# A decoder layer on one core: the self-attention's matrix products reordered in phases of eight, with three score banks

## The chip, the cores and the metric

The kernel runs on one core of a Trainium2 chip. The time is device microseconds of one execution; the runs' median is compared. Before the change three runs gave 863.48, 863.65 and 865.51 us.

The engines of a core work through their own instruction streams and wait for each other by semaphores: PE (TensorE) multiplies matrices into PSUM, DVE (VectorE), ACT (ScalarE) and POOL (GpSimd) work elementwise, SP issues DMAs. PSUM has eight banks of 128 x 512 float32. POOL is given no PSUM operand in this kernel.

## The reference

A decoder layer over x (2 x 1024 x 256), 16 heads of 16:

```python
q, k, v = (x @ W.T for W in (Wq, Wk, Wv))                 # split over the heads
attn = softmax(q @ k.T / sqrt(16)) @ v                     # 1024 keys, no mask
x = layernorm(x + attn)
x = layernorm(x + cross_attention(x, ctx, mask))           # 77 keys
x = layernorm_affine(x + top2_experts(x))                  # 8 experts, 256 -> 512 -> 256
```

The change lies in the second line, and in the projections of q and k that run beside it.

## The kernel before, in words

**Units.** The self-attention is cut into 16 units: batch (2) x group of four heads (4) x half of the queries (2, 512 each). Each unit has 32 steps, one for each key tile of 128 (8) and head (4). A step is a score matmul (`scores`, L534, bfloat16 parts stacked to 98 rows), an exponential on ACT (`exps`, L1488) and a value product (`values`, L542, float32). Value products of four heads go to the four 32-column strips of the array and add up in bank 6; four heads of one key tile form a group. The values carry a column of ones, so the softmax's sum comes with them.

**Maxima.** The softmax needs each query's maximum first. For each unit PE computes 16 pairs of matmuls of 128 queries x 1024 keys (`max_pair`, L515) into `quad`, banks 0 to 3, two banks to a pair, and DVE reduces each pair (`reduce_max`, L952). After the 16th, DVE negates (`negate`), PE turns the result (`turn_negmax`, L528, into bank 7), DVE copies it (`keep_negrows`, L965), SP puts it into two rows of `qstack` (`load_negmax`), and the score matmul subtracts it. Pairs run ahead: during unit u, PE computes pairs 8 to 15 of unit u+1 and 0 to 7 of unit u+2.

**Results.** When a unit's value products are in bank 6, ACT copies it (`outT`, L1571), PE turns it (`turn_out`, L721, into bank 7) and DVE divides by the sums (`normalise`, L1214).

**Late projections.** q and k come from 16 projections ("jobs", `project`, L466) of which 8 run early and one in each of units 1 to 8, into bank 7. Each is split in three bfloat16 parts: ACT copies the high one (`high`), DVE makes the rest, the middle and the low one (`split_rest`, `split_mid`, `split_low`). SP stores the parts (`store_parts`) and loads them as stacks for two units at a time (`load_group`), after the odd unit's last value product.

**Order.** It is written out by hand in PE's `unit` (L724): eight times a group of four scores, four maximum matmuls (two pairs) and four value products of the group before. Scores alternate between banks 4 and 5; `probs` holds 8 tiles. The maximum matmuls alternate with the scores one by one.

After unit 15, whose stream already holds the first cross-attention work (`turn_x1`, `project_q2`, `scores2`), come cross-attention and the experts. Meanwhile POOL has split the experts' weights from the end of the last projection on.

Names in the profile: `bank` stands for banks 4 to 7 and `quad` for 0 to 3.

Of the kernel before, what the change touches and what calls it, by code (L numbers as in the profile page):

```python
# [13 lines left out]
P = 128  # L14
# [14 lines left out]
PR = 8  # L29
# [45 lines left out]
def build(nc, t):  # L75

    with ExitStack() as ctx:
# [154 lines left out]
        neg_loaded = sem("neg_loaded")  # L232
        scores_ready, probs_ready, probs_used = map(sem, ("scores_ready", "probs_ready", "probs_used"))
# [43 lines left out]
        START2 = (2, 3, 5)  # L277

# [11 lines left out]
        QK_BANK = [(4, 5, 0, 1)[n % 4] if n < EARLY_JOBS else 7 for n in range(QK_JOBS)]  # L290

        def job_of(u):
            n = EARLY_JOBS - 1 + u
            return n if EARLY_JOBS <= n < QK_JOBS else None

# [20 lines left out]
        def _(sp):  # L316
# [22 lines left out]
            def store_parts(n):  # L339
# [3 lines left out]
                for part in range(3):  # L343
                    if part == 0:
                        sp.wait_ge(hi_done, n + 1)
                    elif part == 1:
# [45 lines left out]
            def sp_unit(it, k, last):  # L392
# [64 lines left out]
        def _(pe):  # L457
            def project(n, c):
# [7 lines left out]
                mm = pe.matmul(bank[QK_BANK[n]], w_in[("wq", "wk")[w]][:, c, half * P:half * P + P], xT[:, c, g * 512:g * 512 + 512],  # L466
# [41 lines left out]
            def max_pair(u, k, p, halves=(0, 1)):  # L508

                slot, half, j, qt = unit_slot(k), k % 2, p // 4, p % 4  # L510
                if 0 in halves:
                    pe.wait_ge(max_taken, u * 16 + p + 1)
                q = qstack[slot][0:MAXROW, half, j, qt * P:qt * P + P]
                for e in halves:
                    mm = pe.matmul(bank[2 * (p % 2) + e], q, kstack[slot][0:MAXROW, j, e * 512:e * 512 + 512],  # L515
# [4 lines left out]
            def turn_negmax(u, k, first=False):  # L520
                if first:
                    pe.wait_ge(v_done, V_JOBS)
                else:
                    pe.wait_ge(o_normed, u)
                if u and job_of(u - 1) is not None:
                    pe.wait_ge(rest_done, job_of(u - 1) + 1)
                pe.wait_ge(neg_parts, u + 1)
                pe.transpose(bank[7].bitcast(BF16)[0:32, 0:P], negparts[:, k % 2, :], ident16[:, :]).then_inc(neg_turned, 1)  # L528

            def scores(u, k, i):  # L530

                slot, half, kt, j = unit_slot(k), k % 2, i // 4, i % 4
                pe.wait_ge(probs_ready, u * STEPS + i + 1)
                mm = pe.matmul(bank[4 + i % 2], kstack[slot][0:KROWS, j, kt * P:kt * P + P],  # L534
# [4 lines left out]
            def values(u, k, i):  # L539
                kt, j = i // 4, i % 4  # L540
                pe.wait_ge(probs_ready, u * STEPS + i + 3)
                pe.matmul(bank[6][32 * j:32 * j + VW, :], v_all[:, u // 2, kt, j, :], probs[:, i % PR, :],  # L542
                          start=(kt == 0), stop=(kt == KT - 1), skip_group_check=True).then_inc(probs_used, 1)
# [24 lines left out]
            turn_negmax(0, 0, first=True)  # L568
# [3 lines left out]
            for i in range(3):  # L572
# [17 lines left out]
            def project_q2(g, half):  # L590
                if half == 0:
                    pe.wait_ge(x1T_done, g * 2 + 2)
                for c in range(C2):
# [115 lines left out]
            pairs = [(1, p) for p in range(AHEAD, 16)] + [(2, p) for p in range(AHEAD - 1)]  # L709
            when = [pairs[2 * m:2 * m + 2] for m in range(KT)]  # L710
            pairs0 = [(1, p) for p in range(AHEAD0, 16)] + pairs[16 - AHEAD:]
            when0 = [pairs0[3 * m:3 * m + 3] for m in range(4)] + [pairs0[12 + 2 * m:14 + 2 * m] for m in range(4)]
            SPREAD = (1, 2, 1)
            TURN, TURN0 = 5, 6

            def turn_out(u):
                pe.wait_ge(o_copied, u + 2)
                pe.wait_ge(neg_rows, min(u + 2, UNITS))
                pe.wait_ge(o_normed, u + 1)
# [1171 lines left out]
```

## Time and profile before

| | |
|---|---|
| median of 3 runs | 863.65 us |
| span of the profiled execution, first to last instruction | 856.1 us |
| what lies around the span, median less span | 7.5 us |
| PE busy | 737.2 us (86%) |
| DVE busy | 638.0 us (75%) |
| ACT busy | 488.0 us (57%) |
| POOL busy | 305.1 us (36%) |

The execution that was profiled has no time of its own beside its span in the results; the median stands for it. Busy is the time in which an engine has an instruction in flight, so a share of 86% does not say that PE streams at its peak. A row of the timeline merges equal instructions that follow each other; its bracket gives the idle time before it and which engine's work ended that idle time. In a row with x2 the second starts inside the time given. PEclk is the granted TensorE clock as a share of 2.4 GHz.

### The profile page before, as it was taken

What the parts mean: (1) busy time and instruction counts of PE and PEld (TensorE: products, weight loads), DVE (VectorE), ACT (ScalarE), POOL (GpSimd) and SP (SyncE); (2) the same over time, 40 slices, a digit from 0 to 9 for tenths busy, and PEclk for the clock granted to TensorE, in tenths of its full rate; (3) what the DMA queues carried; (4) which work ended last, traced back from release to release, by engine and by line L of the source; (5) the groups of instructions that cost most, each with busy time, mean ns of one, the idle gap of its engine ahead of it and who ended that gap; (6) DMA issues with size and microseconds to landing.
All of it is one profiled execution on the core that took longest, in us unless ns stands there. A gap on an engine that the chain in (4) does not pass through costs nothing.

```text
span 856.1 us, 14502 instructions
## 1 busy us (share of the span) xinstructions
PE 737.2 (86%) x4572; PEld 355.0 (41%) x4572; DVE 638.0 (75%) x1087; ACT 488.0 (57%) x982; POOL 305.1 (36%) x249
## 2 busy tenths in 40 slices
PE   6789999999999999999988889899869898789800
PEld 3442222222222222222223356566657676567600
DVE  3488888888888888777884779897927656589765
ACT  2225677777777677776776553442335666457622
POOL 8000600000000398890002465555732474444311
PEclk9898999999999999999999999897979999899965
DMA  7746040030401699883000090000141332413121
GB/s 197 185 111 159 5 94 20 19 77 17 93 20 35 147 254 276 249 258 115 2 1 1 17 375 2 0 2 1 49 148 40 92 128 89 145 48 95 58 99 49
DMA packets 51170, 80.72 MB, mean 94 GB/s; under 512 B 16469, under 2 KB 35416, under 8 KB 49690
## 3 DMA queue, kind: packets, MB, share of 16 engines
q1 hardware_dynamic: 37065, 44.91, 19.2%
q0 software_dynamic: 9952, 31.29, 11.9%
q10 hardware_dynamic: 4080, 3.61, 1.8%
q8 instruction: 40, 0.66, 0.3%
q14 instruction: 33, 0.26, 0.1%
HBM read 48.21 MB, written 33.11 MB: 95 GB/s over the span
## 4 chain that ended last, share of the span: by engine, by line
PE 57%; DVE 20%; DMA 6%; issue 5%; ACT 4%; POOL 4%; SPq 2%; DVEq 1%; ACTq 0%; POOLq 0%
PE bank L542 12%; PE bank L534 12%; PE quad L515 11%; PE quad L861 5%; DVE rowmax L952 5%; PE bank L878 5%; DMA kstack<-k_parts 3%; PE quad L612 2%; PE bank L466 2%; DVE hl L1182 2%; ACT probs L1488 2%; POOL x_sorted L1778 2%; DVE sc L1055 1%; DVE max L1062 1%; DMA qstack<-q_parts 1%
## 5 line engine op out<-in xcount | busy, mean ns | idle before, releaser
L952 DVE TENSOR_REDUCE rowmax<-quad 128x1 f32<-128x1024 f32 x256 | 303.1, 1219 | 75.9 <-PE quad L515 75.4
L1488 ACT ACTIVATE probs<-bank 128x512 f32<-128x512 f32 x512 | 284.2, 595 | 115.1 <-PE bank L534 112.2
L534 PE MATMUL bank<-qstack,kstack 98*128 98x512 bf16 x512 | 194.1, 387 | 11.7 <-ACT probs L1488 10.0
L515 PE MATMUL quad<-kstack,qstack 96*128 96x512 bf16 x512 | 177.7, 387 | 15.5 <-DVE rowmax L952 6.7
L861 PE MATMUL quad<-xbT,w 128*128 128x128 bf16 x1104 | 119.6, 224 | 22.5 <-DVE hl L1182 16.1
L542 PE MATMUL bank<-probs,v_all 128*32 128x512 f32 x1024 | 139.0, 611 | 0.0
L534 PEld LDWEIGHTS bank<-qstack,kstack 98*128 98x128 bf16 x512 | 49.0, 97 | 191.7 <-ACT probs L1488 162.8
L861 PEld LDWEIGHTS quad<-xbT,w 128*128 x1104 | 91.3, 100 | 53.1 <-issue 38.3
L1612 ACT ACTIVATE hid<-quad,b 128x128 f32<-128x128 f32 x184 | 52.6, 370 | 59.6 <-PE quad L861 58.0
L515 PEld LDWEIGHTS quad<-kstack,qstack 96*128 96x128 bf16 x512 | 48.5, 99 | 77.0 <-DVE rowmax L952 39.3
L1832 POOL DMA_INDIRECT y_tokens<-ysb,dest x46 | 47.3, 1029 | 82.8 <-DVE ysb L1196 75.1
L1730 POOL DMA_DIRECT2D w1raw<-in_w x8 | 6.5, 806 | 188.6 <-PE bank L466 188.6
L878 PE MATMUL bank<-w,hh 128*128 x184 | 71.8, 392 | 1.5 <-DVE hl L1182 1.4
L1182 DVE TENSOR_TENSOR hl<-hid,hh 128x512 bf16<-128x512 f32 x46 | 42.9, 933 | 25.2 <-ACT hh L1618 25.2
L1766 POOL TENSOR_TENSOR lnv<-lnv,power 128x4 f32<-128x4 f32 (+1 forms) x14 | 19.1, 1367 | 110.2 <-DVE lnv L1007 110.2
L1786 POOL TENSOR_TENSOR sc<-sc,max 128x1232 f32<-128x1232 f32 x15 | 34.4, 2291 | 55.1 <-DVE max L1062 55.1
L878 PE MATMUL bank<-w,hl 128*128 x184 | 51.4, 279 | 0.0
L1509 ACT ACTIVATE pT<-bank 128x512 f32<-128x512 f32 (+1 forms) x48 | 23.6, 524 | 41.3 <-PE bank L630 41.1
L612 PE MATMUL quad<-kbd,q2T 128*128 128x308 f32 x128 | 43.5, 475 | 1.3 <-DVE sc L1055 1.3
L644 PE MATMUL bank<-pT,vbd 128*128 128x512 f32 (+3 forms) x100 | 37.6, 528 | 2.4 <-ACT pT L1509 2.4
L1055 DVE TENSOR_TENSOR sc<-quad,cap 128x1232 f32<-128x1232 f32 x16 | 22.8, 1428 | 22.4 <-PE quad L612 22.4
L1778 POOL DMA_INDIRECT x_sorted<-attn_all,rowof x32 | 32.8, 1025 | 12.1 <-issue 8.0
(181 smaller groups left out, 984.6 us busy)
## 6 DMA issues: line engine op xcount, KB each, us to landing
xb<-x_sorted SPq DMA_DIRECT2D x46, 129.0 KB, 2.3
x_sorted<-blank POOLq DMA_DIRECT2D x6, 774.0 KB, 9.1
w1raw<-in_w POOLq DMA_DIRECT2D x8, 512.0 KB, 6.0
w2raw<-in_w POOLq DMA_DIRECT2D x8, 512.0 KB, 6.4
w_split<-w1two POOLq DMA_DIRECT2D x8, 512.0 KB, 5.7
w_split<-w2two POOLq DMA_DIRECT2D x8, 512.0 KB, 4.4
w<-w_split SPq DMA_DIRECT2D x16, 256.0 KB, 5.0
w<-w_split SPq DMA_DIRECT2D x4, 1024.0 KB, 11.7
```

What stands on the lines that cost most here:

```text
L515: mm = pe.matmul(bank[2 * (p % 2) + e], q, kstack[slot][0:MAXROW, j, e * 512:e * 512 + 512], start=True, stop=True)
L534: mm = pe.matmul(bank[4 + i % 2], kstack[slot][0:KROWS, j, kt * P:kt * P + P], qstack[slot][0:KROWS, half, j, :], start=True, stop=True)
L542: pe.matmul(bank[6][32 * j:32 * j + VW, :], v_all[:, u // 2, kt, j, :], probs[:, i % PR, :], start=(kt == 0), stop=(kt == KT - 1), skip_gr ...
L612: mm = pe.matmul(bank[e][:, 0:4 * SC], q2T[:, half, i * P:i * P + P], kbd[:, g // 2, half, 4 * (e % 2):4 * (e % 2) + 4, :].rearrange("p h ...
L861: mm = pe.matmul(bank[m % 3][:, fc * P:(fc + 1) * P], w1[half][c][fc][:, bass.ds(at, P)], xbT[:, m % 3, 2 * part + c, :], start=(k == 0), ...
L878: mm = pe.matmul(bank[Y_BANK[m % 2]][:, 0:n], a[:, m % 2, fc, :], w2[fc][:, bass.ds(at * (2 * D // P), n)], start=(step == 0), stop=(fc == ...
L952: dve.tensor_reduce(rowmax[:, k % 2, p:p + 1], quad[:, 2 * (p % 2):2 * (p % 2) + 2, :].rearrange("p a n -> p (a n)"), AX_X, ALU.max).then_ ...
L1182: dve.tensor_tensor(hl[:, m % 2, :, :], hid[:, m % 2, :, :], hh[:, m % 2, :, :], ALU.subtract).then_inc(hl_done, 1)
L1488: act.activation(probs[:, i % PR, :], bank[4 + i % 2], ACT.Exp, scale=INV4).then_inc(probs_ready, 1)
L1612: act.activation(hid[:, m % 2, fc, :], bank[m % 3][:, fc * P:(fc + 1) * P], ACT.Relu, bias=b1[:, bass.ds(e, 1), fc]).then_inc(hid_done, 1)
L1778: pool.indirect_dma_start(xs[h], bass.IndirectOffsetOnAxis(ap=rowof[:, j, n:n + 1], axis=0), xsend[:, n, :], None).then_inc(scattered[h], 16)
L1832: pool.indirect_dma_start(ys[h], bass.IndirectOffsetOnAxis(ap=dest[:, m % XB:m % XB + 1], axis=0), ysb[:, m % YB, :], None, bounds_check=2 ...
```

## The change

- PE's unit is four phases in place of eight groups. A phase is eight times a score and one half of a maximum pair (in unit 0 at first a whole pair), then the value products of two key tiles, eight in one block. `probs` holds 12 tiles.
- Scores rotate over banks 4, 5 and 7, and three run ahead of the exponentials (LEADING).
- `turn_out` and `turn_negmax` now write to banks 2 and 0. So that they fit into the rotation of the pairs, pairs 2 to 9 use the other two banks than before, from unit 2 on: `turn_out` comes after pair 9, `turn_negmax` after pair 1, and pairs 10 and 2 wait for one reduction more.
- A late projection runs in one piece after score 14, in the score bank that is next in turn. ACT copies its bank twice, as the bfloat16 part and in float32 (`keep_job`), and POOL makes the rest, the middle and the low part, before its masks and before the experts' weights.
- A value product raises `probs_used` once for four.
- SP loads the next stacks after the odd unit's last score matmul instead of its last value product.
- The cross-attention work in unit 15 has new places in the order.

```diff
-PR = 8
+PR = 12
+PHASES, PER = 4, 8
+LEADING = 3
+JOB_AT = 14
...
+        SCORE_BANKS = (4, 5, 7)
+        NEG_BANK, OUT_BANK = 0, 2
...
+        def score_bank(u, i, job=False):
+            before_it = sum(job_of(v) is not None and (v, JOB_AT) < (u, i) for v in range(u + 1))
+            return SCORE_BANKS[(u * STEPS + i + before_it + job) % len(SCORE_BANKS)]
...
# SP, load_group of the next stacks
-                    sp.wait_ge(probs_used, u * STEPS + (STEPS + PR))
+                    sp.wait_ge(scores_ready, u * STEPS + STEPS)
...
# PE
             def max_pair(u, k, p, halves=(0, 1)):
+                shifted = u >= 2 and 2 <= p < 10
                 if 0 in halves:
-                    pe.wait_ge(max_taken, u * 16 + p + 1)
+                    if u >= 2 and p == 3:
+                        pe.wait_ge(neg_rows, u)
+                    elif u >= 2 and p == 11:
+                        pe.wait_ge(o_normed, u)
+                    else:
+                        pe.wait_ge(max_taken, u * 16 + p + 1 + (u >= 2 and p in (2, 10)))
...
+            def turn_negmax(u, k):
...
+                elif u < UNITS - 1:
+                    pe.wait_ge(max_taken, u * 16 + 19)
...
+            def turn_out(u):
+                pe.wait_ge(o_copied, u + 2)
+                if u < UNITS - 2:
+                    pe.wait_ge(max_taken, u * 16 + 43)
...
+            def scores(u, k, i):
+                behind = i - JOB_AT if job_of(u) is not None else 0
+                if behind == LEADING:
+                    pe.wait_ge(raw_done, job_of(u) - EARLY_JOBS + 1)
                 else:
+                    pe.wait_ge(probs_ready, u * STEPS + i + 1 + (0 < behind < LEADING))
...
+            def values(u, k, h):
+                if h == 0:
+                    pe.wait_ge(o_copied, u + 1)
+                pe.wait_ge(probs_ready, u * STEPS + PER * h + PER + LEADING)
+                for i in range(PER * h, PER * h + PER):
+                    kt, j = i // GH, i % GH
+                    mm = pe.matmul(bank[6][32 * j:32 * j + VW, :], v_all[:, u // 2, kt, j, :], probs[:, (u * STEPS + i) % PR, :],
+                                   start=(kt == 0), stop=(kt == KT - 1), skip_group_check=True)
+                    if j == GH - 1:
+                        mm.then_inc(probs_used, GH)
...
# PE, ahead(i)
                         scores(u, k, i)
+                        if i == JOB_AT and job_of(u) is not None:
+                            pe.wait_ge(probs_ready, u * STEPS + i + 2)
+                            for c in range(C2):
+                                project(job_of(u), c)
...
# PE, unit
+                    max_pair(u + a, k + a, p, (e,))
+                    if (a, p, e) == (1, 9, 1) and u:
+                        turn_out(u - 1)
+                    elif (a, p, e) == (2, 1, 1):
                         turn_negmax(u + 1, k + 1)
...
+                for h in range(PHASES):
+                    for s in range(PER):
+                        ahead(PER * h + LEADING + s)
+                        share = -(-len(halves) // (PER * (PHASES - h) - s))
+                        for a, p, e in halves[:share]:
+                            pair(a, p, e)
+                        halves = halves[share:]
...
+                    values(u, k, h)
...
# ACT, after exponential 14 of a unit with a job
+            def keep_job(u):
+                act.activation(parts[:, n % RING, 0, :], bank[job_bank(u)], ACT.Copy).then_inc(hi_done, 1)
...
+                act.activation(rest[:, n % 2, :], bank[job_bank(u)], ACT.Copy).then_inc(raw_done, 1)
...
# POOL
+            for n in range(EARLY_JOBS, QK_JOBS):
+                m, raw, three = n - EARLY_JOBS + 1, rest[:, n % 2, :], parts[:, n % RING, :, :]
+                pool.wait_ge(raw_done, m)
+                pool.tensor_tensor(raw, raw, three[:, 0, :], ALU.subtract).then_inc(late_rest, 1)
+                pool.wait_ge(late_rest, m)
+                pool.tensor_copy(three[:, 1, :], raw).then_inc(late_mid, 1)
+                pool.wait_ge(late_mid, m)
+                pool.tensor_tensor(three[:, 2, :], raw, three[:, 1, :], ALU.subtract).then_inc(late_low, 1)
```

## Rows read from the trace of the kernel before

**Rows 1.** The page: chain that ended last, shares of the span by engine

```profile
PE 57%; DVE 20%; DMA 6%; issue 5%; ACT 4%; POOL 4%; SPq 2%; DVEq 1%; ACTq 0%; POOLq 0%
```

**Rows 2.** Busy time by window: us, busy (instructions), PEclk, DMA share, GB/s

```profile
61.58:92.81 31.23, 29.40 (x140) 7.82 (x141) 24.48 (x24) 19.42 (x35) 5.58 (x3) 0.89 0.50 113
92.81:275.68 182.87, 179.51 (x960) 53.34 (x959) 150.56 (x169) 132.13 (x239) 8.35 (x5) 1.00 0.19 42
275.68:303.68 28.00, 25.73 (x138) 7.60 (x137) 23.64 (x24) 18.88 (x34) 11.19 (x10) 1.00 0.64 153
303.68:453.11 149.43, 141.78 (x785) 39.75 (x784) 118.77 (x146) 109.25 (x199) 75.23 (x64) 1.00 0.55 160
404.31:428.70 24.39, 23.91 (x134) 6.79 (x133) 19.91 (x21) 18.17 (x33) 0.00 (x0) 1.00 0.01 1
453.11:487.68 34.57, 30.20 (x138) 11.05 (x136) 18.62 (x27) 21.75 (x37) 12.06 (x8) 0.95 0.00 1
```

**Rows 3.** Timeline, unit 13: start, us, engine line op; x2 merges two

```profile
423.21 0.39 PE L534 MATMUL bank<-qstack,kstack 98*128 98x512 bf16 x1
...
423.64 2.17 ACT L1488 ACTIVATE probs<-bank 128x512 f32<-128x512 f32 x4 [0.71 <-PE bank L534]
...
423.88 0.59 PE L515 MATMUL quad<-kstack,qstack 96*128 96x512 bf16 x2
...
424.30 2.36 DVE L952 TENSOR_REDUCE rowmax<-quad 128x1 f32<-128x1024 f32 x2 [0.53 <-PE quad L515]
...
424.78 0.39 PE L534 MATMUL bank<-qstack,kstack 98*128 98x512 bf16 x1
...
425.10 1.06 PE L542 MATMUL bank<-probs,v_all 128*32 128x512 f32 x8
...
426.10 0.39 PE L534 MATMUL bank<-qstack,kstack 98*128 98x512 bf16 x1
```

**Rows 4.** Timeline, unit 0

```profile
77.50 0.60 PE L515 MATMUL quad<-kstack,qstack 96*128 96x512 bf16 x2
...
78.14 3.49 DVE L952 TENSOR_REDUCE rowmax<-quad 128x1 f32<-128x1024 f32 x3 [0.41 <-PE quad L515]
...
79.42 0.60 PE L515 MATMUL quad<-kstack,qstack 96*128 96x512 bf16 x2 [0.45 <-DVE rowmax L952]
```

**Rows 5.** Timeline, ends of units 13 and 15

```profile
427.50 1.07 PE L542 MATMUL bank<-probs,v_all 128*32 128x512 f32 x8
...
428.70 0.60 ACT L1571 ACTIVATE outT<-bank 128x512 f32<-128x512 f32 x1 [0.51 <-PE bank L542]
...
486.60 0.14 PEld L542 LDWEIGHTS bank<-probs,v_all 128*32 128x32 f32 x2 [0.61 <-ACT probs L1488]
...
487.68 0.60 ACT L1571 ACTIVATE outT<-bank 128x512 f32<-128x512 f32 x1 [1.14 <-PE bank L542]
```

**Rows 6.** Chain of waits, unit 1: start us, us, what

```profile
95.42 0.44 PE bank L721 x4
...
99.51 0.42 DVE attn_all L1222
...
101.95 0.86 PE bank L466 x2
```

**Rows 7.** POOL's early split, by line (ns: min/median/max); DVE's cast, timeline of unit 8

```profile
L1692 POOL TENSOR_TENSOR parts<-rest,parts x4: 1148/1156/1158, 14.1 to 18.7; 128x512 bf16<-128x512 f32 x4
...
295.61 2.30 DVE L926 CAST parts<-rest 128x512 bf16<-128x512 f32 x1
```

**Rows 8.** Waits of PE (310 to 480); chain, units 9 to 10; POOL's timeline

```profile
PE quad L515 <- DMA kstack<-k_parts: 2.5, 2, 1.4
...
328.94 0.60 SPq L362
...
331.73 11.20 DMA kstack<-k_parts
...
450.60 1.68 POOL L1766 TENSOR_TENSOR lnv<-lnv,power 128x8 f32<-128x8 f32 x1 [62.99 <-DVE lnv L1007]
```

More of the change, by code:

```diff
@@ L567, in _ @@
             max_pair(1, 1, 0)
-            turn_negmax(0, 0, first=True)
+            turn_negmax(0, 0)
             for p in range(1, AHEAD0):
@@ L571, in _ @@
             pe.wait_ge(neg_loaded, 32)
-            for i in range(3):
+            for i in range(LEADING):
                 scores(0, 0, i)
@@ L706, in rank @@
                 mm.then_inc(ranks_ready, 1)
[L709 to L719, printed above, removed]
-                for qt in range(4):
-                    tr = pe.transpose(bank[7][:, qt * P:qt * P + P], outT[:, qt * P:qt * P + P], ident[:, :])
-                tr.then_inc(o_turned, 1)
+            pairs = [(1, p) for p in range(AHEAD, 16)] + [(2, p) for p in range(AHEAD)]
+            pairs0 = [(1, p) for p in range(AHEAD0, 16)] + [(2, p) for p in range(AHEAD)]
             def unit(it, k, last):
@@ new lines, in pair @@
+                    if (a, p, e) == (1, 9, 1) and u:
+                        turn_out(u - 1)
+                    elif (a, p, e) == (2, 1, 1):
+                        turn_negmax(u + 1, k + 1)
+                halves = [(a, p, e) for a, p in (pairs if u else pairs0) for e in range(2)]
+                for h in range(PHASES):
[5 more added lines that the diff above has]
+                        halves = halves[share:]
+                        if last and s == 3:
+                            if k == 2 and h == 2:
+                                turn_negmax(u + 1, k + 1)
+                            elif k == 3 and h == 0:
+                                turn_out(u - 1)
+                                turn_x1(0)
+                            elif k == 3 and h == 1:
+                                for half in range(2):
+                                    scores2(0, half)
@@ L777, in unit @@
                             pe.wait_ge(mask_step, MASK_STEPS)
-                        elif m in START2:
+                        elif h < 3:
                             for half in range(2):
-                                scores2(START2.index(m), half)
-                heads(KT - 1)
-                if not (last and k + 2 > 3):
-                    max_pair(u + 2, k + 2, AHEAD - 1)
-                ahead(STEPS + 2)
+                                scores2(h, half)
+                    values(u, k, h)
             for it in range(3):
@@ L951, in reduce_max @@
                 dve.wait_ge(max_ready, u * 16 + p + 1)
-                dve.tensor_reduce(rowmax[:, k % 2, p:p + 1], quad[:, 2 * (p % 2):2 * (p % 2) + 2, :].rearrange("p a n -> p (a n)"),
+                at = 2 * ((p + (u >= 2 and 2 <= p < 10)) % 2)
+                dve.tensor_reduce(rowmax[:, k % 2, p:p + 1], quad[:, at:at + 2, :].rearrange("p a n -> p (a n)"),
                                   AX_X, ALU.max).then_inc(max_taken, 1)
```

115 lines of the change are left out of this document (46 added, 69 removed).

## The prediction

> **What bounds the kernel now.** I read the page's chain that ended last first: TensorE (PE) holds 57% of it, VectorE (DVE) 20% [rows 1]. Then the stretches [rows 2]. Self-attention runs as 16 units from 61.6 to 487.7 us. A unit without a late projection takes 24.39 us (unit 13, 404.31 to 428.70), one with it 26.12 (units 1 to 7, 182.87 us for seven), and PE is busy in all but half a microsecond of each; DVE has 19.9 and 21.5 us of work in them, ScalarE (ACT) under 19. So the matmul stream seems the bound. The timeline says what the stream is made of and how close DVE is behind it. In a regular group of four score matmuls (S), four maximum matmuls (M, two make a pair) and four value products (V) [rows 3], S and M lie 0.22 us apart, V starts 0.32 after its S, and the next S is 1.00 after V starts. A V group thus costs 1.10, and the whole group 4 x 0.22 + 4 x 0.22 + 1.10 = 2.86; measured 2.89 (423.21 to 426.10). DVE takes up a pair 0.42 after the pair's second M starts (its second M at 423.88, the reduction at 424.30); two reductions take 2.36, that is 1.13 from start to start and 1.22 for the last. DVE rests for 0.53 per group. ACT starts an exponential 0.43 after its S and does four in 2.17: 0.525 apart, 0.60 long.
>
> The four quad banks hold two pairs, so the third of a burst waits until the first is reduced. Unit 0 has three pairs to a group and shows it [rows 4]: pair A is issued at 77.50 and 77.72, its reduction starts at 78.14 and ends at 79.36; pair C could go at 78.81 and goes at 79.42, 0.06 after that end. I use this spacing below.
>
> **Eight value products together.** Two groups of four now stand back to back. The last value product of the attention, alone because its exponential came late, ran from 486.60, and ACT could read its bank at 487.68 [rows 5]; after a full group of four that is 1.20 (427.50 to 428.70). So the four heads stream side by side, in about 0.86 us, 0.04 apart. The second four use the same columns of the array and must stream after the first: 0.10 entry + 0.14 stagger + 2 x 0.86 = 1.96, against 2.20 for two groups. Bounds: 1.82 (no stagger) and 2.20 (nothing saved). I take 1.96, since the stagger is in the row. TensorEngine Tiling in the Trainium skill (Key Properties) says that changing the tiling mode drains the engine. The trace agrees with its 0.32 in place of 0.22; that rule is on the change's side, though the lone transpose of the maxima, which used to lie against a V group, now pays two switches. TensorE: Matmul & The Clock Gate in the Trainium skill (The cost: per-tile semaphore tail) prices each increment at 26.3 ns; six fewer per block would give an estimate of 1.80 for it and a total near 871.
>
> **One phase of eight.** A phase is now S M eight times, then the block. Count from its first S; Sn is the phase's nth S, Mna and Mnb the two matmuls of pair n (0 to 3). M0b is at 0.66, so reduction R0 starts at 1.08, ends at 2.30; R1 starts at 2.21, ends at 3.43. M2a could go at 1.98 but needs R0: 2.35. Then S 2.57, M2b 2.79, S 3.01; M3a needs R1: 3.48. S 3.70, M3b 3.92, block 4.14, next phase 6.10. Without the wait it would be 3.52 + 1.96 = 5.48. R2 and R3 end at 4.56 and 5.69 and DVE then idles until 7.18, as no new pair can appear during the block. The cycle M0b - R0 - R1 - M3 - block - M0b is closed: 0.42 + 1.13 + 1.22 + 0.05 + 0.66 + 1.96 + 0.66 = 6.10. Two old groups take 5.78. This is my central claim: the longer block starves DVE and then the burst of four pairs outruns two buffers. Three score banks keep ACT clear: exponentials run from 0.42 every 0.525, and the eighth S needs the end of the fifth's, 3.12, before 3.70.
>
> **The transposes.** turn_out now sits between pair 1 and pair 2 in bank 2 and waits for R0: 2.35. It lasts 0.44, by the chain of waits [rows 6]: S 2.79. Pair 2 must now wait for R1, 3.48 (banks 0 and 1): S 3.70, M2b 3.92, S 4.14, M3a 4.36 (normalise follows R1 and ends with a product of 0.42 [rows 6], at about 4.15), S 4.58, M3b 4.80, block 5.02, end 6.98. turn_negmax has the same place in the third phase; its few tenths lie within the wait for R1, and keep_negrows (0.2) before M3a too: again 6.98. A unit is 6.98 + 6.10 + 6.98 + 6.10 = 26.16, against 24.39.
>
> **Late projections (units 1 to 8).** They now stand whole behind S14, the fourth S of the second phase, for 1.72 us (two times 0.86 [rows 6]). They need exponential 12 of the unit: start 1.61. M1b moves to 3.33, S to 3.55. ACT makes two copies where it made one, at 3.53 and 4.06 to 4.66, so the S behind them in that bank waits to 4.72; pair 3 waits for R1 (3.75 to 4.97, so 5.02), its neighbour S for ACT's exponential 15, 5.245. Block 5.69, end 7.65: 1.55 over a plain phase. Unit: 27.71, against 26.12. DVE loses its three splits, but it idles here anyway, so that is worth nothing, except in unit 8: there a cast took 2.30 us while GpSimd (POOL) ran, and the unit took 28.00, 1.88 more than its seven forerunners [rows 2, 7]. SBUF — State Buffer in the Trainium skill (Who interferes with whom) says a cast of DVE can be blocked by GpSimd and tensor_reduce on trn2 never is; the trace agrees (units 9 to 13 keep their length although POOL works through most of them). POOL's own splits: two subtractions of 1.15 [rows 7] and a cast no longer than that, under 3.5 us per unit, after which SP stores; the next reader is the stack load a unit later. POOL gets to its masks only after unit 8, and so to the experts' weights later, by the length of the masks and the shift of unit 8, together less than a unit and a half; it idles 62.99 us before its next work at 450.60 [rows 8], which covers that. Uncovered, the excess over 63 us would delay the cross-attention; I see none.
>
> **Stack loads.** SP now issues them once the unit's last S is issued, about 4.3 us before the unit's end, instead of after its last value products. The PE waits for kstack, 2.5 us in all in units 10 and 12 [rows 8], go: 14.0 us of issue and transfer (328.94 to 342.93) now lie under 4.3 + 6.98 + 6.10 = 17.4 us. On its queue the load is moved past nothing; the row of maxima follows it half a unit later. This gain is already in my 26.16.
>
> **Unit 0** has 42 halves. First phase: eight pairs at DVE's 1.13, first reduction about 64.2 (the granted clock of the unit was 0.89 on average, it began at the lower level, so issue is slow at first, but DVE sets the pace), pair 7's M at 71.2, end 73.7. Second, five pairs: 7.1, then 6.98 and 6.10: 93.9 against 92.7. +1.2. **Unit 14** lacks pairs in its second half, where ACT's 8 x 0.525 and the block set the length: 6.98 + 6.10 + 5.5 + 5.4 = 24.0. **Unit 15** has no M and holds the first cross-attention work. Laid out the same way, with ACT's exponentials, the two copies of x1T and of q2T and the last block of 1.96 behind the last exponential, it comes to 34.9 against 34.57 [rows 2].
>
> **Sum.** Units 1 to 7: 7 x 1.59 = 11.1. Unit 8: -0.3. Units 9 to 14: 5 x 26.16 + 24.0 = 154.8 against 149.43 [rows 2], +5.4. Units 0 and 15: +1.2 + 0.3. Total +17.7: the profiled span goes from 856.1 to 873.8. The median of the runs is 863.65; the 7.5 us around the span I leave alone. Forecast 881.4. A block of 1.82 takes 0.14 from some 62 phases, 8.7: 872.7. One of 2.20 adds 14.9: 896.3.
>
> **Rivals.** (1) Faster: PE's stream is the bound, as its busy time says. Place: pairs 2 and 3 of each phase; it decides if their waits are absent, so that phases average under 6.1 us (24.4 / 4). A unit is then 64 x 0.22 + 4 x 1.96 + 0.44 + 0.3 = 22.7, or 24.4 with a projection: 7 x 1.7 + 3.6 + 149.43 - 5 x 22.7 - 24.0 = 27.4 less, 836. For it: DVE has only 20 us of work in a 24 us unit. Against: unit 0's wait [rows 4] is this very pattern. (2) No change: waits half as long as laid out, paid for by the stack loads (2.5) and unit 8 (1.9): about 864. (3) The blocks save nothing, since the second four heads drain before loading: 896 or more; for it speaks only that no row shows eight together. (4) PE's clock, 1.00 in units 1 to 14 [rows 2], falls to 1.2 GHz in places because PE waits more (0.62 us in a plain phase). The 0.95 of unit 15 is such a dip; there PE was busy for 30.2 of 34.6 us, a share that the new units come near to. A unit wholly at 1.2 GHz would double its 22.7 us of issue, so one to two such units in all give 900 to 920.
>
> **Chances.** Forecast 0.75, (1) 0.10, (2) 0.04, (3) 0.08, (4) 0.03. About 0.3% is what a measurement can tell from no change. Faster 0.10, same 0.04, slower 0.86. Range 866 to 898: both bounds of the block, and some room below for terms laid out by hand; case 1 is left out.
>
> **What would show it.** In a plain phase M of pair 2 idles some 0.4 us and of pair 3 some 0.2 before a release by DVE's reduction, phases last 6.1 and 7.0, units 26.2 and 27.7; DVE idles about 1.5 us at each block; the kstack waits and the long cast are gone; a block starts the next S 1.86 after its own start. Wrong: units under 24.4, ACT named as releaser of most S, or blocks far from 1.86.

## The result, and the profile after

The changed kernel takes 888.0 us (median of 4 runs, 884.08 to 890.32), beside 863.57 for the kernel before (4 runs, 859.94 to 865.51). The ratio is 1.0289, 95% interval 1.0257 to 1.0321: slower by 24.4 us, where the forecast was 881.4, slower by 17.7. The profiled execution took 886.86 us, its span is 885.0.

First the page of the changed kernel: busy times, the chain that ended last, and three groups (busy us, mean ns of one | idle before, releaser).

```profile
PE 736.3 (83%) x4572; PEld 367.6 (42%) x4572; DVE 626.0 (71%) x1063; ACT 476.3 (54%) x990; POOL 330.4 (37%) x273
...
PE 51%; DVE 26%; issue 6%; DMA 5%; ACT 5%; POOL 3%; SPq 1%; DVEq 1%; ACTq 0%; another core or an unknown queue 0%; POOLq 0%
...
L976 DVE TENSOR_REDUCE rowmax<-quad 128x1 f32<-128x1024 f32 x256 | 299.6, 1218 | 109.6 <-PE quad L536 109.1
...
L536 PE MATMUL quad<-kstack,qstack 96*128 96x512 bf16 x512 | 194.5, 390 | 26.0 <-DVE rowmax L976 17.5
...
L580 PE MATMUL bank<-probs,v_all 128*32 128x512 f32 x1024 | 126.1, 611 | 2.2 <-ACT probs L1505 2.2
```

In the chain DVE goes from 20 to 26% and PE from 57 to 51% [rows 1]. On the page of the kernel before, the reductions idled 75.9 us and the maximum matmuls 15.5 us; now it is 109.6 and 26.0, and each names the other as releaser. Two engines that wait for each other by turns are a closed cycle, and neither one's busy share (83% and 71%) shows it. PE's busy time is what it was, 736 for 737.

The stretches, in the columns of [rows 2]: units 1 to 7, unit 9, units 10 to 14, unit 13, unit 15, and 3.2 us within unit 9.

```profile
94.27:288.63 194.36, 179.25 (x960) 59.10 (x959) 141.10 (x147) 128.18 (x245) 20.50 (x21) 1.00 0.19 42
...
316.40:346.15 29.75, 25.44 (x134) 7.81 (x133) 21.49 (x21) 17.33 (x33) 24.91 (x22) 0.94 0.78 209
346.15:474.93 128.78, 116.37 (x650) 36.65 (x649) 97.44 (x123) 86.67 (x165) 62.53 (x52) 1.00 0.54 155
425.25:451.42 26.17, 23.79 (x134) 7.61 (x133) 19.71 (x21) 17.44 (x33) 0.00 (x0) 1.00 0.01 1
474.93:509.96 35.03, 28.78 (x137) 11.32 (x135) 20.71 (x29) 19.80 (x36) 13.82 (x9) 0.95 0.00 1
342.30:345.50 3.20, 3.20 (x18) 0.60 (x16) 1.80 (x2) 0.80 (x2) 2.33 (x3) 0.50 1.07 269
```

Unit 13 takes 26.17 us (24.39 before), with DVE's work 0.2 us less and PE idle for 2.4 us instead of 0.5 [rows 2].

A plain phase, the answer to [rows 3], unit 13 of the changed kernel:

```profile
432.09 0.39 PE L568 MATMUL bank<-qstack,kstack 98*128 98x512 bf16 x1
...
433.18 4.62 DVE L976 TENSOR_REDUCE rowmax<-quad 128x1 f32<-128x1024 f32 x4 [1.35 <-PE quad L536]
...
433.85 0.38 PE L568 MATMUL bank<-qstack,kstack 98*128 98x512 bf16 x1
...
434.46 0.39 PE L536 MATMUL quad<-kstack,qstack 96*128 96x512 bf16 x1 [0.23 <-DVE rowmax L976]
...
435.12 0.38 PE L568 MATMUL bank<-qstack,kstack 98*128 98x512 bf16 x1
...
435.59 0.39 PE L536 MATMUL quad<-kstack,qstack 96*128 96x512 bf16 x1
...
436.34 1.92 PE L580 MATMUL bank<-probs,v_all 128*32 128x512 f32 x16
...
438.20 0.39 PE L568 MATMUL bank<-qstack,kstack 98*128 98x512 bf16 x1
```

Read the starts rather than the brackets. Without a wait a matmul follows its neighbour by 0.22. The first half of pair 2 follows by 0.61 (433.85 to 434.46), that of pair 3 by 0.47 (435.12 to 435.59): 0.64 us of waiting per phase, of which the bracket shows 0.23, since a matmul counts as busy for 0.38 and so hides what follows it. The block starts the next score 1.86 after its own start. The phase lasts 6.11 and DVE rests 1.35 ahead of it.

This is where the 22.3 us went by which the attention (to the last copy out of bank 6) is longer in these two traces (it ends at 487.68 and at 509.96):

| | before | after | more | forecast |
|---|---|---|---|---|
| unit 0, end | 92.81 | 94.27 | 1.5 | 1.2 |
| units 1 to 7 | 182.87 | 194.36 | 11.5 | 11.1 |
| unit 8 | 28.00 | 27.77 | -0.2 | -0.3 |
| units 9 to 14 | 149.43 | 158.53 | 9.1 | 5.4 |
| unit 15 | 34.57 | 35.03 | 0.5 | 0.3 |

Behind the attention the two kernels have the same code, which took 368.4 us before and 375.0 after. I don't put that down to the change: in the 14 traces of this study it took 368.1 to 378.6 us, and the kernels that ran together on a chip lie together (368.1 to 371.6 the first four, 377.1 to 378.6 the next four, 373.2 to 376.2 the next three), whatever was done to the attention. For single stages I therefore compare units, for totals the ratio of runs side by side.

### The profile page after: what moved, and what is told of

It reads as the page before. It is cut to its first block, busy times and chain, and to the rows that moved or that the text cites. A ratio compares the mean times of both kernels' runs of the same rounds, so it can differ in the third digit from the quotient of the medians.

```text
span 885.0 us, 14500 instructions
## 1 busy us (share of the span) xinstructions
PE 736.3 (83%) x4572; PEld 367.6 (42%) x4572; DVE 626.0 (71%) x1063; ACT 476.3 (54%) x990; POOL 330.4 (37%) x273
## 4 chain that ended last, share of the span: by engine, by line
PE 51%; DVE 26%; issue 6%; DMA 5%; ACT 5%; POOL 3%; SPq 1%; DVEq 1%; ACTq 0%; another core or an unknown queue 0%; POOLq 0%
DVE rowmax L976 14%; PE bank L580 13%; PE quad L536 9%; PE bank L568 8%; PE quad L884 5%; PE bank L901 4%; PE quad L654 2%; PE bank L481 2%; DVE hl L1206 2%; PE bank L686 2%; DMA qstack<-negrows 2%; POOL x_sorted L1817 2%; DMA qstack<-q_parts 1%; DVE sc L1079 1%; ACT probs L1505 1%
## 5 line engine op out<-in xcount | busy, mean ns | idle before, releaser
L976 DVE TENSOR_REDUCE rowmax<-quad 128x1 f32<-128x1024 f32 x256 | 299.6, 1218 | 109.6 <-PE quad L536 109.1
L1505 ACT ACTIVATE probs<-bank 128x512 f32<-128x512 f32 x512 | 270.2, 604 | 125.3 <-PE bank L568 123.7
L536 PE MATMUL quad<-kstack,qstack 96*128 96x512 bf16 x512 | 194.5, 390 | 26.0 <-DVE rowmax L976 17.5
L580 PE MATMUL bank<-probs,v_all 128*32 128x512 f32 x1024 | 126.1, 611 | 2.2 <-ACT probs L1505 2.2
L1739 POOL TENSOR_TENSOR rest<-rest,parts 128x512 f32<-128x512 f32 x8 | 9.3, 1157 | 255.9 <-ACT rest L1517 255.9
L580 PEld LDWEIGHTS bank<-probs,v_all 128*32 128x32 f32 x1024 | 27.1, 110 | 69.2 <-issue 48.2
L1817 POOL DMA_INDIRECT x_sorted<-attn_all,rowof x32 | 32.8, 1024 | 17.3 <-issue 5.5
```

What stands on the lines that cost most here:

```text
L536: mm = pe.matmul(bank[2 * ((p + shifted) % 2) + e], q, kstack[slot][0:MAXROW, j, e * 512:e * 512 + 512], start=True, stop=True)
L580: mm = pe.matmul(bank[6][32 * j:32 * j + VW, :], v_all[:, u // 2, kt, j, :], probs[:, (u * STEPS + i) % PR, :], start=(kt == 0), stop=(kt ...
L976: dve.tensor_reduce(rowmax[:, k % 2, p:p + 1], quad[:, at:at + 2, :].rearrange("p a n -> p (a n)"), AX_X, ALU.max).then_inc(max_taken, 1)
L1505: act.activation(probs[:, n % PR, :], bank[score_bank(u, i)], ACT.Exp, scale=INV4).then_inc(probs_ready, 1)
L1817: pool.indirect_dma_start(xs[h], bass.IndirectOffsetOnAxis(ap=rowof[:, j, n:n + 1], axis=0), xsend[:, n, :], None).then_inc(scattered[h], 16)
```

## The experiments

Two numbers carry most verdicts: the length of a plain unit (copy of bank 6 to copy of bank 6; of units 9 to 13 the shortest, so the one that nothing disturbed) and of a unit with a projection. Before they are 24.4 and 26.12, after 26.17 and 27.77. Undisturbed units repeat to a few hundredths of a microsecond within a trace and from one to the next, while totals vary by 0.5%.

### Is it the length of the block?

```diff
-PHASES, PER = 4, 8
+PHASES, PER = 8, 4
```

Everything else of the change stays: three banks, transposes in the rotation, splits on POOL, early load. (Unit 15's work is put at the same step numbers.)

> The changed kernel with blocks of four value products again (eight phases of four slots); three score banks, transposes in the rotation of the maximum, GpSimd's splits and the early stack loads stay. Theory T (the block of eight starves VectorE, and four pairs in a row then outrun the two pairs of quad banks): a plain stretch of eight slots falls from 6.11 to 2 x 2.86 = 5.72 us; turn_out and turn_negmax still wait about 0.6 for a reduction, so a unit is 6.75 + 5.72 + 6.5 + 5.72 = 24.7 without a projection and some 26.6 with one, instead of 26.17 and 27.77. Total near 866. Rival A (the transposes and their extra waits in the rotation are the loss, the block is innocent): units stay above 25.7, total above 880. Rival B (what is left is the late projection in one piece): only units 9 to 14 get near the old 24.4, units 1 to 8 stay near 27.7.

Measured: 858.38 us beside 858.84, ratio 1.0009 (0.9984 to 1.0034). Plain unit 24.47 (unit 13; units 9 to 12 took 24.70 to 25.36), projection unit 26.31. The theory had 24.7 and 26.6. The same groups of its page:

```profile
L977 DVE TENSOR_REDUCE rowmax<-quad 128x1 f32<-128x1024 f32 x256 | 302.0, 1220 | 89.5 <-PE quad L536 88.6
...
L536 PE MATMUL quad<-kstack,qstack 96*128 96x512 bf16 x512 | 192.6, 386 | 10.6 <-DMA qstack<-q_parts 7.1
...
L580 PE MATMUL bank<-probs,v_all 128*32 128x512 f32 x1024 | 137.5, 608 | 1.4 <-ACT probs L1506 1.4
```

The value products are busy for 11.4 us more (137.5 for 126.1), and yet the attention ends at 486.37, 23.6 us sooner: on the page no wait for reductions leads for the maximum matmuls any more (10.6 us of idle time, most of it for a transfer, for 26.0), and DVE idles 20 us less before its reductions (89.5 for 109.6). The block's length is the cause of the loss. One unit was odd: unit 8 took 32.25 us.

```profile
290.28 4.40 POOL L1748 TENSOR_SCALAR cap<-cap 128x1232 f32<-128x1232 int32 x1
290.42 4.30 DVE L984 TENSOR_SCALAR negparts<-rowmax 128x16 bf16<-128x16 f32 x1
...
296.12 0.29 PE L548 MATMUL quad<-ident,negparts 128*32 128x128 bf16 x1 [4.41 <-DVE rowmax L977]
```

A negation of 16 columns, 0.17 us by itself, stood for 4.30 beside a mask operation of POOL's, and PE idled 4.41 before `turn_negmax`, with the granted clock at 0.50 for the next 4 us. The bracket names the reduction, which had to wait for the negation; what held the negation is POOL's row. The experiments on POOL below follow this up.

### Is it DVE, or PE's stream?

```diff
# changed kernel; the same in the kernel before
-quad[:, at:at + 2, :].rearrange("p a n -> p (a n)")
+quad[:, at, :]
```

Each reduction reads 512 of the 1024 keys, so the maxima are of half the keys.

> The changed kernel with reductions over the first 512 of each pair's 1024 keys only (the second maximum matmul runs, its half is not read; a softmax may be shifted by any number). A reduction should take about 0.65 us in place of 1.22. Theory T: the waits of pair 2 and pair 3 go, a plain phase is 16 x 0.22 + 0.09 + 1.86 = 5.47 plus 0.1 that ScalarE takes = 5.57; with the transposes 6.2 and 5.9; unit 23.2, with a projection 24.8; unit 0 gains some 4; total 840 to 848. Rival (TensorE's own stream or its drains are the loss, VectorE is only a symptom): phases stay near 6.1, total above 875.

> The kernel before with the same half reduction. Theory T: TensorE's stream bounds it, VectorE is close behind only in unit 0 (0.6 per group) and around normalise (0.37): a unit goes from 24.4 to 24.0, unit 0 loses 4 to 5, total 851 to 857. So e2 must be FASTER than e3 by some 10 us: blocks of eight are worth their 0.25 us per phase once VectorE is out of the way. Rival (the block of eight gains nothing in itself): e2 and e3 equal, or e2 slower.

Measured: after 841.24 us, ratio 0.9814 (0.9777 to 0.9852); before 850.78, ratio 0.9900 (0.9859 to 0.9942). Plain units 23.28 and 24.08, projection units 25.44 and 25.72. With a reduction of 0.69 us the changed kernel waits no more for DVE in plain phases, and it wins by 0.80 a unit. So blocks of eight do save PE what they should, and the loss is DVE's. The totals say it less cleanly than the units: of the 8.5 us by which the attention ends sooner in the changed kernel (468.84 for 477.33), 5.3 are that units 9 to 12 of the kernel before were disturbed in its trace (unit 10 took 27.82) and those of the changed kernel hardly. Only the projection unit was off, 25.44 for 24.8 expected: 2.16 over the plain one, where the four matmuls take 1.72 of the stream. Two scores behind ACT's copies come 0.28 late together; what makes the rest stays open.

### What is the third score bank worth?

```diff
-LEADING = 3
+LEADING = 2
-        SCORE_BANKS = (4, 5, 7)
+        SCORE_BANKS = (4, 5)
```

> The changed kernel with two score banks (4 and 5), two scores ahead; blocks of eight and all else stay. Theory T: ScalarE's exponentials then hold each score back to 0.525 us, but VectorE's wait is the longer one: scores S0 to S7 of a phase at 0, 0.44, 1.08, 1.60, 2.13, 2.65, 3.18, 3.73, pair 3 at 3.51 as before, block at 4.2 instead of 4.14. A plain phase goes from 6.11 to about 6.15, total 886 to 892: the third bank buys almost nothing here. Rival (the third bank matters, without it the new order would lose more): each phase 0.3 or more longer, total over 905.

Measured: 904.84 us, ratio 1.0568 (1.0526 to 1.0611), a miss in the total. Beside a kernel before of 863.65 that ratio is 912.7, where 886 to 892 was expected and the rival had over 905. The waits of PE in this kernel from 94 to 500 us (in total, times, longest), which takes in the first 10 us of unit 15, then those of the changed kernel from 94 us to the end of unit 14:

```profile
PE quad L536 <- DVE rowmax L976: 13.0, 27, 0.6
PE bank L568 <- ACT probs L1505: 7.1, 22, 1.1
PE bank L568 <- ACT rest L1517: 4.2, 8, 0.5
```

```profile
PE quad L536 <- DVE rowmax L976: 14.7, 46, 0.6
PE quad L557 <- DVE rowmax L976: 7.5, 14, 0.5
PE quad L548 <- DVE rowmax L976: 6.4, 13, 1.1
PE bank L568 <- ACT probs L1505: 0.7, 3, 0.3
```

To the end of unit 14 alone the second row is 4.9 us in 19 waits. The plain phase is the same (6.12 us, for 6.11), as expected: DVE sets it. But the phase with `turn_out` grows to 7.38 and that with `turn_negmax` to 7.18 (both 6.98), units with a projection to 29.4, and unit 15, where ACT paces, to 41.2 (35.0). The attention ends at 531.55, 21.6 us later: so much is the third bank worth. The rival was right on the total, and wrong on the plain phases. I had priced the bank only where it does nothing.

### Can the starved start of a phase be filled?

```diff
-share = -(-len(halves) // (PER * (PHASES - h) - s))
+share = (2, 0, 2, 0, 2, 0, 0, 2)[s] if u else -(-len(halves) // (PER * (PHASES - h) - s))
```

The two halves of a pair follow each other, so a pair is ready 0.2 us after its first half.

> The changed kernel; from unit 1 on, the two matmuls of a maximum pair stand side by side in the phase of eight: S0 MM S1 S2 MM S3 S4 MM S5 S6 S7 MM, then the block of eight. Nothing is added or removed. Theory T (closed cycle: pair 0's second matmul, two reductions, pair 3, block): the second matmul of pair 0 moves from 0.66 to 0.44, so R0 runs 0.86 to 2.08, R1 1.99 to 3.21, pair 3 at 3.40, block at 3.94: a plain phase is 5.80 instead of 6.11, one with a transpose 6.75 instead of 6.98, a unit 25.1 instead of 26.17, one with a projection 26.7 instead of 27.77. In all some 15 us under the changed kernel: 1.011 to 1.016 of the kernel before. Rival (the loss is drains, or queueing in TensorE, whatever the order of the maximum's matmuls): units stay at 26.2, ratio 1.026 or more.

Measured: 883.58 us, ratio 1.0228 (1.0191 to 1.0265): the total misses the 1.011 to 1.016 that was worked out, and by itself its interval doesn't exclude the rival's 1.026. The units do exclude it. The plain phase is 5.81 (5.80 worked out), one with `turn_negmax` 6.75 (6.75), one with `turn_out` 6.87, and the plain unit 25.23, 0.1 over what was worked out. The attention ends at 501.65, 8.3 us sooner instead of some 15. The projection unit, 27.41, missed its 26.7: as in the half reduction, ACT's second copy holds a score (2.5 us in eight units, by the waits). Units 9 to 11 were disturbed (25.81 to 26.79), and unit 15 took 36.74. The plain phases confirm the cycle: shorten one of its links, from phase start to the first full pair, and each phase shrinks.

### Two repairs of the kernel before

```diff
# SP, before the next stacks: both kernels of this pair
-sp.wait_ge(probs_used, u * STEPS + (STEPS + PR))
+sp.wait_ge(scores_ready, u * STEPS + STEPS)
# POOL, before the weights: the second alone
-pool.wait_ge(qk_ready, QK_JOBS)
+pool.wait_ge(parts_done, QK_JOBS - 4)
```

> The kernel before with one part of the change: SP loads the next stacks after the odd unit's last score matmul instead of its last value product. Theory: PE's two waits for kstack at the middle of units 10 and 12 (2.5 us in the trace) go, nothing else moves: units 10 and 12 from 25.7 and 25.9 to 24.4, total 2 to 3 us less, ratio about 0.997. Rival: the loads then lie beside the experts' weights and delay the rows of maxima; no change.

> e6, and GpSimd starts on the experts' weights only when VectorE has made the last part of the last projection, some 10 us later. Theory: the cast of 2.30 us in unit 8 goes back to 0.42, unit 8 from 28.0 to 26.1; together with the early load 4 to 5 us less than before, ratio 0.994 to 0.996. Rival: GpSimd's later start pushes the weights' traffic onto something else, or another short VectorE cast is caught: the gain of e6 alone or less.

Measured: 865.19 us, ratio 1.0004 (0.9986 to 1.0022), and 862.76, ratio 0.9992 (0.9968 to 1.0015). In the traces both mechanisms work. The early load takes units 10 and 12 from 25.66 and 25.90 to 25.15 and 24.40 (24.4 was expected of both, and unit 11 gives 0.4 back). The later start of POOL takes unit 8 from 28.00 to 26.12. The attention ends 5.5 us sooner with both (482.22), 3.4 of it in units 8 to 14 and 1.2 in unit 15, where the granted clock was 1.00 instead of 0.95. Unit 9 is longer, 25.85 for 24.66. The totals can't be told from no change, and the 0.994 to 0.996 expected of both repairs lies just outside the interval: what 3 us in seven units do to the total these runs can't show, since the interval of twelve runs spans 4.

### Keeping POOL away from the negation

In the kernel with blocks of four, POOL's masks are first moved ahead of its late splits.

> e1 (the changed kernel with blocks of four) with GpSimd's masks ahead of its late splits, as in the kernel before, instead of behind them. In e1, unit 8 took 32.25 us: VectorE's negate of 128 x 16 took 4.30 beside GpSimd's first mask operation (4.40), and TensorE waited 4.41. Theory: this is a block between the two engines and goes with the order: unit 8 at 26.3, total 5 to 6 us under e1, so 0.992 to 0.995 of the kernel before, faster than both kernels. Rival: the wait has another cause (stores of the parts, the row's DMA) and unit 8 stays over 30.

Measured: 864.02 us, ratio 0.9981 (0.9961 to 1.0002). Unit 8 falls from 32.25 to 26.53, as expected (26.3). The total does not: 0.992 to 0.995 was expected, and the interval holds no change. Now unit 10 takes 27.73:

```profile
339.77 2.14 POOL L1785 TENSOR_TENSOR w2two<-w2raw,w2two 128x1024 bf16<-128x1024 f32 x1
339.95 1.99 DVE L986 SCALAR_TENSOR_TENSOR negparts<-rowmax,negparts 128x16 bf16<-128x16 f32 x1
...
343.13 0.23 PE L548 MATMUL quad<-ident,negparts 128*32 128x128 bf16 x1 [2.09 <-DVE rowmax L977]
```

The other half of the negation meets a weight split. So next the weight splits are spaced by the arrival of the maxima's rows:

```diff
                 for k in range(2):
+                    pool.wait_ge(neg_loaded, 32 * (10 + (2 * e + k) // 3))
+                    if k == 0:
+                        fill_sorted(e // FILLS, e % FILLS)
                     split_weights(e, k)
```

It is put into three kernels: blocks of four, the changed kernel itself (with the masks first), and the kernel before (with both repairs).

> The changed kernel with blocks of four and GpSimd's masks first, and GpSimd lets three weight splits (and the fill of the sorted rows) follow each time the maxima's rows have landed, from unit 9's on, in place of all in a row. Theory: what is left in units 10 to 12 over 24.47 us comes from DVE's negation standing behind a GpSimd split (1.99 us measured) and from the fills beside the rows' transfer. Then units 9 to 13 take 24.5 each, the last copy out of bank 6 ends at 479 us (483.4 without the spacing, 487.7 in the kernel before), ratio to the kernel before 0.988 to 0.994. Rival: the excess is the stacks' late arrival, which GpSimd doesn't touch: unit 10 stays at 27 us, attention ends at 482 to 484, ratio 0.996 to 1.000.

> The changed kernel (blocks of eight) with GpSimd's masks first and its weight splits spaced in the same way. Theory: unit 9's 29.75 us in the changed kernel is 26.2 of the plain unit and 3.6 of collisions with GpSimd (negation 1.95, the rows' transfer 6.90 in place of 1.7, the clock's dip behind it). It falls to 26.2, unit 10 to 26.2, the attention ends at 505 to 506.5 (509.96), the ratio to the kernel before is 1.020 to 1.026 (1.0289). Rival: it belongs to the change of kind of unit (the last projection's stacks): unit 9 stays above 28.

> The kernel before with the early load and the wait on the copies (as in the run with both), and GpSimd's weight splits spaced in the same way. Theory: unit 9 falls from 25.85 to 24.4, the attention ends at 480.8 (482.2 without the spacing, 487.7 in the kernel before), ratio to the kernel before 0.991 to 0.996. Rival: the spacing pushes GpSimd's work against the norm in unit 15: that unit grows from 33.35 and the ratio is 1.00.

Measured, all three beside 865.58 us: blocks of four 859.61, ratio 0.9932 (0.9909 to 0.9956); the changed kernel 883.98, ratio 1.0216 (1.0181 to 1.0250); the kernel before 861.67, ratio 0.9959 (0.9939 to 0.9979). All three ratios are in what the theory expected. The stages bear it out for the changed kernel only.

In the changed kernel units 9 to 13 are all 26.17 or 26.18 now: the collisions are gone (the negation takes 0.17 to 0.28 there), and the interval holds the ratio of the forecast (881.4 / 863.65 = 1.0206). Its attention ends at 507.16, a little past what I expected, because unit 15 took 36.6. There eight matmuls of the cross-attention took 3.51 us, where they had taken 2.24, with the granted clock at 0.81 from 494 to 501 on average; that is 1.3 of the 1.6 us by which the unit is longer than in the changed kernel (the first row is of this kernel's timeline, the second of the changed kernel's):

```profile
494.07 3.51 PE L654 MATMUL quad<-kbd,q2T 128*128 128x308 f32 x8
```

```profile
498.27 2.24 PE L654 MATMUL quad<-kbd,q2T 128*128 128x308 f32 x8
```

In the other two kernels unit 9 came right (24.60 and 24.41) and unit 10 did not (27.41 and 25.79), so their attention ended at 484.34 and 483.93, where 479 and 480.8 were expected, and no sooner than without the spacing (483.43 and 482.22). In blocks of four the unit and the end of the attention are about what the rival had named (27, and 482 to 484), though not for its reason, the stacks, while the ratio is the theory's. What made these two ratios better than those without the spacing (0.9981 and 0.9992) the traces of the attention don't show, and it can't be credited to the spacing. In blocks of four the weights' fetch was late, and the third split of its portion met the negation:

```profile
339.54 1.04 POOL L1783 CAST w2two<-w2raw 128x1024 bf16<-128x1024 f32 x1 [3.49 <-DMA w2raw<-in_w]
340.66 2.12 POOL L1785 TENSOR_TENSOR w2two<-w2raw,w2two 128x1024 bf16<-128x1024 f32 x1
...
341.16 1.66 DVE L984 TENSOR_SCALAR negparts<-rowmax 128x16 bf16<-128x16 f32 x1
```

One more kernel put only two splits into the first portion.

```diff
-pool.wait_ge(neg_loaded, 32 * (10 + (2 * e + k) // 3))
+pool.wait_ge(neg_loaded, 32 * (10 + (2 * e + k + 1) // 3))
```

> As the run with blocks of four and spaced splits, but only two splits stand in the first portion, so that the fetch of the weights, which came 4 us late in unit 10 beside the last stacks, no longer pushes the third split of a portion onto the negation (1.66 us in place of 0.17, PE idle 1.76 before the turn, and the granted clock at 0.79 behind it). Theory: unit 10 falls from 27.4 to 24.5 to 25.0, the attention ends at 481 to 482 (484.3), ratio to the kernel before 0.988 to 0.993. Rival: unit 10's excess is the stacks' transfer at a DMA share of 1.0: it stays above 26.5, ratio 0.993 to 0.996.

Measured: 855.17 us beside 858.52, ratio 0.9963 (0.9941 to 0.9984). The attention ends at 481.88, as expected; the total misses its 0.988 to 0.993, unit 10 is 25.70 for 24.5 to 25.0, and unit 12 is 25.96, where the negation took 1.83. In unit 10 the fetch was late again, by 5.08 us, and another split met the negation:

```profile
338.56 1.04 POOL L1783 CAST w1two<-w1raw 128x1024 bf16<-128x1024 f32 x1 [5.08 <-DMA w1raw<-in_w]
339.68 2.12 POOL L1785 TENSOR_TENSOR w1two<-w1raw,w1two 128x1024 bf16<-128x1024 f32 x1
340.25 1.58 DVE L984 TENSOR_SCALAR negparts<-rowmax 128x16 bf16<-128x16 f32 x1
```

A spacing by starts doesn't hold where a transfer decides when the split begins. A wait after each fetch, put between the negation's two ends, would; it wasn't tried. The two kernels of blocks of four with spaced splits are faster than the kernel before, by their intervals 0.2 to 0.9%, and so faster than the changed one; which of the two is better stays open.

## Why the prediction was right, and where its sizes were off

**The block, 1.96 with its entry.** Right: 0.31 from the matmul before (436.03 is the last maximum matmul's start in the phase shown, the block's is 436.34), less the usual 0.22, plus 1.86 to the next score: 1.95. The rival that the blocks save nothing is out. The estimate of 1.80 by the Trainium skill's increments (TensorE: Matmul & The Clock Gate, The cost: per-tile semaphore tail) is not borne out: six increments fewer left the block where the heads' stagger alone puts it.

**Pairs outrun DVE.** Right: the second pair of a phase to wait stood at 3.50 from the first score (3.48 forecast), the first at 2.37 (2.35), the phase is 6.11 (6.10), and DVE rests at each block. Halving the reduction removes the loss, blocks of four remove it, and closing the pairs shortens it by what the cycle says. That PE's stream is the bound (the fastest rival, 836) is excluded: its own condition, pairs 2 and 3 without waits, was nearly met only where half the keys were reduced (a plain phase of 5.45), at 841. The no-change rival needed waits half as long as laid out, and they are as long as laid out.

**The transposes.** Right. The third phase of unit 13, to its next score 6.98 later, rows of the changed kernel:

```profile
440.56 0.23 PE L548 MATMUL quad<-ident,negparts 128*32 128x128 bf16 x1 [0.44 <-DVE rowmax L976]
...
441.69 0.39 PE L536 MATMUL quad<-kstack,qstack 96*128 96x512 bf16 x1 [0.58 <-DVE rowmax L976]
...
445.18 0.39 PE L568 MATMUL bank<-qstack,kstack 98*128 98x512 bf16 x1
```

**Late projections.** Right to 0.06 per unit (27.77 for 27.71). The projection started 1.57 after its phase's first score (1.61), the phase took 7.70 (7.65). POOL's splits are hidden as forecast, 3.07 us, 216.93 to 220.00, though the negation at 219.50 took 0.53 beside them; PE did not wait for it.

```profile
213.75 1.98 PE L481 MATMUL bank<-xT,wqkv 128*128 128x512 f32 x4
...
215.77 0.60 ACT L1512 ACTIVATE parts<-bank 128x512 bf16<-128x512 f32 x1 [1.09 <-PE bank L481]
...
216.26 0.59 ACT L1517 ACTIVATE rest<-bank 128x512 f32<-128x512 f32 x1
...
216.93 1.16 POOL L1739 TENSOR_TENSOR rest<-rest,parts 128x512 f32<-128x512 f32 x1 [24.69 <-ACT rest L1517]
...
218.84 1.16 POOL L1743 TENSOR_TENSOR parts<-rest,parts 128x512 bf16<-128x512 f32 x1
```

**Units 9 to 14: the term that was too small,** +9.1 for +5.4. The working had 5 x 26.16 + 24.0. Three units gave 26.17 and unit 14 gave 23.51, but unit 9 took 29.75 and unit 10 26.75. I had looked for POOL's effect on DVE in one large cast, and concluded from a constant length of units 9 to 13 that POOL's weights hurt nothing. That reading was wrong: before, they took 24.66, 25.66, 24.41, 25.90 and 24.39. The stacks' waits are in units 10 and 12, but in unit 9 the negation took 0.95. The small negation was exposed to POOL all along, and the sum put this at nothing. In unit 9 of the changed kernel:

```profile
328.77 2.12 POOL L1783 TENSOR_TENSOR w2two<-w2raw,w2two 128x1024 bf16<-128x1024 f32 x1
328.98 1.95 DVE L983 TENSOR_SCALAR negparts<-rowmax 128x16 bf16<-128x16 f32 x1
...
332.32 0.23 PE L548 MATMUL quad<-ident,negparts 128*32 128x128 bf16 x1 [1.05 <-DVE rowmax L976]
...
341.10 0.39 PE L568 MATMUL bank<-qstack,kstack 98*128 98x512 bf16 x1 [1.40 <-DMA qstack<-negrows]
```

The row of maxima then took its transfer 6.90 us, by the chain of waits:

```profile
328.98 1.96 DVE negparts L983
...
334.16 6.90 DMA qstack<-negrows
...
342.72 3.35 PE bank L580 x16
```

It shares the DMA engines with the weights' traffic and the fill of the sorted rows, issued at 332.63, and PE waited 1.40 for it. Then the granted clock stood at 0.50, the lower level, for the 3.20 us shown with the stretches, and a block took 3.35 in place of 1.86. Negation, transfer and clock together are the 3.6 us over 26.16; the spaced kernel, in which all three are absent, gives 26.17. That POOL's work is their source is shown by it. By the unit's phases they divide so: the third, with the late negation, took 7.59 for 6.98, and the fourth, with the wait for the row and the slow block, 9.06 for 6.11. Which part of POOL's work slowed the transfer, and whether the clock would have fallen without the wait, stays open. The fourth rival, that the clock falls in places, thus happened here, but for 1.5 us, and once more in unit 15, where it had priced 20 or more.

**Unit 0, 15 and 8, the stack loads.** 1.5 for 1.2 (the working took unit 0's end before as 92.7, the trace has 92.81), 0.5 for 0.3, -0.2 for -0.3; the kstack waits are gone from PE's list. In unit 15 the agreement is luck. The working had a last block of 1.96 behind the last exponential, and in the changed kernel it took 3.45:

```profile
506.44 3.45 PE L580 MATMUL bank<-probs,v_all 128*32 128x512 f32 x16 [2.19 <-ACT probs L1505]
```

So the rest of the unit was 1.4 us shorter than laid out. The 34.57 before held a fall of the clock too (0.95 on average): in four other traces with the old order the clock was 1.00 and the unit took 33.35. Against these the changed kernel loses 1.7 us in unit 15, not 0.5.

**Beside the attention.** Of the 24.4 us between the medians 22.3 are the attention's, if the two traces stand for the medians. The rest is within what the same code varies by. My reading of the 7.5 us as what "lies around the span" was wrong: it is 1.9 in the changed kernel's profiled execution (886.86 less 885.0). The 7.5 must have been mostly the difference between a quick profiled execution and the median. It did no harm, because only differences were added to it.

## What to carry to other kernels

Before you lengthen an uninterrupted block on one engine, draw the cycle through its partner. Here four pairs followed a block and two pairs of banks stood between PE and DVE, so the time in which no new work for DVE appeared was paid in each phase, whatever the busy shares said. The same longer blocks with which the kernel lost 2.9% (2.2% with POOL kept away) were worth 0.8 us a unit once the partner was fast enough. And look for tiny instructions on the critical path of an engine that another one can block: give them a time when the other is quiet, or they can cost as much as its longest operation.

## What the runs showed of the hardware

- A DVE operation of 128 x 16 elements, float32 to bfloat16, took 4.30 us beside one POOL operation of 4.40 (blocks of four), and 1.95 and 1.99 beside splits of 2.12 and 2.14, as a TENSOR_SCALAR and as a SCALAR_TENSOR_TENSOR. Alone it takes 0.17. Two reductions beside the same POOL work took 2.36, as always (unit 9 of the changed kernel, 334.32). SBUF — State Buffer in the Trainium skill (Who interferes with whom) names kinds of operations that can block each other, says that the later one is held for the whole of the other's instruction, and excepts tensor_reduce on trn2; these rows agree. What I hadn't expected is how much this costs for one of 16 columns on the critical path.
- Two rows of maxima took 6.90 us to land in a stretch with a DMA share of 0.97 (unit 9 of the changed kernel, 334.16 to 341.05), and 1.7 in the median.
- The granted clock falls for a few microseconds, and not always at the same place in otherwise equal units: unit 15's eight matmuls took 2.24 and 3.51 in two kernels with the same instructions there. PE had idled shortly before each of these falls (1.21 before these eight, 1.40 in unit 9 of the changed kernel, 4.41 in unit 8 with blocks of four), but the same 1.21 stood before the eight that took 2.24, and after an idle of 1.68 in unit 10 of the last kernel the clock stayed at 1.00. One fall came back each time: behind an idle of 1.70 to 2.19, the last block of unit 15 took 3.38 to 3.57 in all five traces with blocks of eight, where a block takes 1.92. What decides it these runs don't show.
